# Four stacked attention layers on one core: a new order of a grouped-query layer's rounds, one moved copy in the layer behind it, and shorter moments

## The reference

```
x = L0(ctx, x)   # latent: keys and values from ctx and x, 16 heads of 32, rmsnorm, MLP
x = L1(x, ctx)   # grouped query: 32 query heads, 8 key heads of 16; layer norm behind; no MLP
x = L2(x, ctx)   # cross: layer norm, 16 heads of 32, layer norm, MLP
x = L3(ctx, x)   # latent again
# L1:
q = hidden @ Wq + bq; k = ctx @ Wk + bk; v = ctx @ Wv + bv
attn = softmax(q @ k.T / 4 + mask)
x = (attn @ v) @ Wo + bo + hidden
return (x - mean(x)) * rsqrt(var(x) + 1e-6) * gamma + beta
```

## Time and profile before

| | |
|---|---|
| median of 3 runs | 2516.99 us (2512.34 to 2518.89) |
| the profiled execution's own time | 2515.64 us |
| its span, first to last instruction | 2513.6 us |
| PE busy, share of the span | 2425.0 us, 96% |
| DVE, ACT, POOL busy | 50%, 43%, 45% |
| mean granted clock of TensorE | 0.991 |

### The profile page before, as it was taken

The page is one execution under the profiler, slowest core; times in us unless marked ns, Lnnn a source line. Parts: engine busy times, 40 slices in busy tenths (PEclk is TensorE's granted clock), DMA queues, the critical chain, the costliest instruction groups (busy, mean ns, idle before and its releaser), DMA issues.

```text
span 2513.6 us, 49031 instructions
## 1 busy us (share of the span) xinstructions
PE 2425.0 (96%) x18400; PEld 2036.1 (81%) x18400; DVE 1256.4 (50%) x3768; ACT 1087.7 (43%) x3688; POOL 1120.8 (45%) x1972
## 2 busy tenths in 40 slices
PE   7999999999999999998898999999999999999999
PEld 6888887888888878877787888888888888788887
DVE  5565655333234676676887333233565555431332
ACT  5555554111114777777887111112555555211111
POOL 3444445600053787878997720042345433740000
PEclk9999999999999999998999999999999999999999
DMA  4221212311034233222454311031121111320100
GB/s 157 69 68 60 97 39 85 97 51 51 1 107 133 75 108 115 99 104 99 172 186 136 119 70 41 11 101 64 35 81 64 52 52 52 110 96 1 51 34 17
DMA packets 107866, 198.36 MB, mean 79 GB/s; under 512 B 9392, under 2 KB 36720, under 8 KB 104688
## 3 DMA queue, kind: packets, MB, share of 16 engines
q1 hardware_dynamic: 107632, 195.22, 23.0%
HBM read 136.47 MB, written 58.72 MB: 78 GB/s over the span
## 4 chain that ended last, share of the span: by engine, by line
PE 79%; ACT 9%; DVE 7%; POOL 4%; DMA 1%; issue 1%; SPq 0%; DVEq 0%; POOLq 0%
PE banks L327 69%; PE banks L468 5%; ACT plain_high L746 5%; PE banks L498 3%; ACT plain_low L746 2%; POOL plain_high L1414 2%; DVE plain_low L1033 1%; DVE stats L1172 1%; PE banks L522 1%; DVE rounded_low L1082 1%; ACT plain_work L730 1%; POOL plain_low L1414 1%; PE banks L359 0%; DMA plain_high<-attention_w 0%; DVE plain_work L1187 0%
## 5 line engine op out<-in xcount | busy, mean ns | idle before, releaser
L327 PE MATMUL banks<-rounded_work,rounded_low 128*128 128x512 f32 (+1 forms) x2688 | 521.1, 348 | 14.5 <-DVE rounded_low L1210 9.1
L839 ACT ACTIVATE plain_work<-banks,columns 128x512 f32<-128x512 f32 x192 | 132.4, 690 | 863.6 <-PE banks L327 863.6
L327 PEld LDWEIGHTS banks<-rounded_work,rounded_low 128*128 128x128 f32 x2688 | 432.9, 192 | 79.3 <-issue 12.5
L327 PE MATMUL banks<-rounded_work,rounded_high 128*128 128x512 f32 (+1 forms) x2400 | 482.3, 355 | 1.8 <-DMA rounded_work<-ctx_split 1.3
L327 PEld LDWEIGHTS banks<-rounded_work,rounded_high 128*128 128x128 f32 x2400 | 396.1, 191 | 67.1 <-issue 5.3
L1383 DVE CAST rounded_work<-plain_work 128x512 fp32r<-128x512 f32 x192 | 106.2, 553 | 687.3 <-ACT plain_work L839 676.6
L1414 POOL TENSOR_SCALAR plain_high<-plain_high,inv_sum 128x128 f32<-128x128 f32 (+1 forms) x768 | 296.8, 409 | 301.6 <-DVE inv_sum L1055 301.3
L327 PE MATMUL banks<-rounded_low,rounded_work 128*128 128x512 f32 x1728 | 416.2, 392 | 0.0
L327 PE MATMUL banks<-rounded_high,rounded_work 128*128 128x512 f32 (+1 forms) x1728 | 391.4, 378 | 0.0
L327 PEld LDWEIGHTS banks<-rounded_low,rounded_work 128*128 128x128 f32 x1728 | 321.4, 188 | 70.7 <-issue 4.4
L327 PEld LDWEIGHTS banks<-rounded_high,rounded_work 128*128 128x128 f32 x1728 | 309.0, 188 | 62.6 <-issue 3.0
(11 more groups left out here) (110 smaller groups left out, 3313.1 us busy)
## 6 DMA issues: line engine op xcount, KB each, us to landing
plain_work<-x SPq DMA_DIRECT2D x96, 256.0 KB, 3.0
plain_work<-mlp_w SPq DMA_DIRECT2D x96, 256.0 KB, 2.7
rounded_work<-ctx_split SPq DMA_DIRECT2D x16, 1024.0 KB, 5.8
u<-plain_work SPq DMA_DIRECT2D x48, 256.0 KB, 2.3
plain_work<-u SPq DMA_DIRECT2D x12, 1024.0 KB, 7.0
x<-plain_work SPq DMA_DIRECT2D x48, 256.0 KB, 2.3
plain_work<-attention_w SPq DMA_DIRECT2D x44, 256.0 KB, 2.6
ctx_split<-rounded_work SPq DMA_DIRECT2D x8, 1024.0 KB, 5.6
```

Of the source, the lines that this page charges most:

```text
L327: mm = pe.matmul(dst, lhs(i), rhs(j), start=first and n == 0, stop=last and n == 2, skip_group_check=True)
L839: act.activation(gelu[:, j % 2, :], bank(key), ACT.Gelu_apprx_tanh, bias=col(m.y, 28 + j)).then_inc(evac_of(key), 1)
```

## The change

What it does, by engine:

- **PE**, second layer: a projection (of the third layer's values, or an output projection) is put between each `pe_scores` and the `pe_turn_probs` behind it. `pe_keys` no longer waits for the hidden rows (`pe_rows` has moved to `pe_queries`), and `pe_values` of the third layer waits for the context, since it is now its first reader.
- **ACT and DVE**, second layer: `act_late_round` and `dve_late_round` take the place of the rounds. The copies of the turned banks come behind exp 1 on ACT, and behind maximum 3 and the first inversion on DVE. Each heads' lo part (`dve_heads`) of rounds 1 and 3 goes into the middle of a later round's maxima. DVE copies both halves of the third layer's values.
- **POOL**: `pool_again` and `pool_root` move from behind round 1's norm to behind round 2's, the biases a round earlier or later.
- **SP**: the context load (`sp_c`) moves from the head of a pair to the end of the one before, behind the stores of keys and values.
- **DVE**, third layer: both copies of turned banks follow maximum 1.
- **Moments**: L1180 and L1181 go, with the wait before them; POOL reads mean and variance from `moments`, and subtracts the mean where it added its negative.

```diff
-                wait_evac(pe, ("X", y.n, p, 0))
-                wait_evac(pe, ("X", y.n, p, 1))
+                if y.kind == LATENT:
+                    pe_rows(pe, y, p)
...
+            if y.kind == GQA and i == 0:
+                pe_rows(pe, y, p)
...
+            if y.kind == CROSS and i == 0:
+                pe.wait_ge(c_loaded, 16 * (c_index(L[1], p) + 1))
...
+        def act_late_round(act, y, p, k, turned, of, between=nothing):
+            act_exp(act, y, p, k, 0)
+            act_exp(act, y, p, k, 1)
+            act_probs(act, of, *turned, 0)
+            act_probs(act, of, *turned, 2)
+            act_exp(act, y, p, k, 2)
+            between()
+            act_exp(act, y, p, k, 3)
...
-            dve.bn_aggr(moments[:, i, :], stats[:, i, :]).then_inc(aggr_done, 1)
-            dve.wait_ge(aggr_done, rt + 1)
+            dve.bn_aggr(moments[:, i, :], stats[:, i, :]).then_inc(aggr_done if y.kind == LATENT else moments_ready, 1)
             if y.kind == LATENT:
+                dve.wait_ge(aggr_done, (B if y.n else 0) + b + 1)
...
-            else:
-                dve.tensor_scalar(neg_mean[:, i:i + 1], moments[:, i, 0:1], -1.0, None, ALU.mult)
-                dve.tensor_copy(spread[:, i:i + 1], moments[:, i, 1:2]).then_inc(moments_ready, 1)
...
+        def dve_late_round(dve, y, p, k, turned, lower, beside, behind, of):
+            dve_max(dve, y, p, k, 0)
+            dve_max(dve, y, p, k, 1)
+            lower()
+            dve_max(dve, y, p, k, 2)
+            beside()
+            dve_max(dve, y, p, k, 3)
+            dve_invert(dve, y, p, k, (0,))
+            dve_probs(dve, of, *turned, 1)
+            dve_probs(dve, of, *turned, 3)
+            behind()
+            dve_invert(dve, y, p, k, (1,))
...
+                dve_late_round(dve, y, p, 1, (p, 0), last_heads, lambda: values(0) if p else None, rows, y)
...
+                dve_late_round(dve, y, p, 2, (p, 1), cross_keys, odd_out, odd_moments, y)
...
+                dve_late_round(dve, y, p, 3, (p, 2), lambda: dve_heads(dve, y, p, 1), lambda: values(1), nothing, y)
...
+                dve_late_round(dve, *((y, p + 1) if more else (L[2], 0)), 0, (p, 3), nothing,
+                               lambda: dve_add(dve, y, 2 * p), even_moments, y)
...
-                for r in range(4):
+                for r in range(2):
                     dve_max(dve, y, p + 1, 0, r)
-                    if r % 2:
-                        dve_probs(dve, y, p, 1, r)
+                dve_probs(dve, y, p, 1, 1)
+                dve_probs(dve, y, p, 1, 3)
+                for r in range(2, 4):
+                    dve_max(dve, y, p + 1, 0, r)
...
                 pool_norm(pool, y, p, 1)
                 if p:
-                    pool_again(pool, y, 2 * p - 2)
-                    pool_root(pool, y, 2 * p - 1)
-                pool_norm(pool, y, p, 2)
-                if p:
-                    pool_again(pool, y, 2 * p - 1)
-                pool_bias(pool, y, 2 * p)
+                    pool_bias(pool, y, 2 * p - 1)
...
+                pool_norm(pool, y, p, 2)
+                if p:
+                    pool_again(pool, y, 2 * p - 2)
+                    pool_root(pool, y, 2 * p - 1)
                 pool_norm(pool, y, p, 3)
-                pool_bias(pool, y, 2 * p + 1)
+                pool_bias(pool, y, 2 * p)
...
+                if p:
+                    pool_again(pool, y, 2 * p - 1)
                 pool_root(pool, y, 2 * p)
+            pool_bias(pool, y, B - 1)
...
+                if more:
+                    sp_ahead(sp, p + 1)
+                if far:
+                    wait_filled(sp, ("V", 1, p + 1, 0))
+                    sp_c(sp, y, p + 2)
```

More of the change, by code:

```diff
@@ L1280, in dve_gqa @@
             dve.wait_ge(m_stored, 64 * GROUPS)
+            for i in range(2):
+                dve_values(dve, L[2], 0, i)
             for p in range(PAIRS):
                 more = p + 1 < PAIRS
-                def inputs():
-                    for i in range(2):
-                        dve_x(dve, *((y, p + 1) if more else (L[2], 0)), i)
-                def next_inputs():
-                    if not more:
-                        for i in range(2):
-                            dve_x(dve, L[2], 1, i)
@@ new lines, in odd_out, with odd_moments, even_moments, rows @@
+                def odd_out():
+                    if p:
+                        dve_add(dve, y, 2 * p - 1)
+                def odd_moments():
+                    if p:
+                        dve_again(dve, y, 2 * p - 2)
+                        dve_added(dve, y, 2 * p - 1)
+                def even_moments():
+                    if p:
+                        dve_again(dve, y, 2 * p - 1)
+                    dve_added(dve, y, 2 * p)
+                def rows():
+                    if more:
+                        for i in range(2):
+                            dve_x(dve, y, p + 1, i)
@@ L1299, in dve_gqa @@
+                dve_late_round(dve, y, p, 1, (p, 0), last_heads, lambda: values(0) if p else None, rows, y)
                 if more:
                     dve_keys(dve, y, p + 1, 0)
-                    dve_keys(dve, L[2], p + 1, 0)
-                dve_round(dve, y, p, 2, (p, 1), nothing)
-                if p:
-                    dve_again(dve, y, 2 * p - 1)
+                else:
+                    for i in range(2):
+                        dve_x(dve, L[2], 0, i)
+                dve_heads(dve, y, p, 0)
@@ L1313, in dve_gqa @@
                 dve_heads(dve, y, p, 2)
-                dve_round(dve, *((y, p + 1) if more else (L[2], 0)), 0, (p, 3), nothing, y)
-                next_inputs()
-                dve_out(dve, y, 2 * p)
+                dve_late_round(dve, *((y, p + 1) if more else (L[2], 0)), 0, (p, 3), nothing,
+                               lambda: dve_add(dve, y, 2 * p), even_moments, y)
                 if more:
                     dve_queries(dve, y, p + 1, 1)
-                dve_heads(dve, y, p, 3)
+                else:
+                    for i in range(2):
+                        dve_x(dve, L[2], 1, i)
+            dve_heads(dve, y, PAIRS - 1, 3)
         def dve_cross(dve, y):
@@ L1441, in pool_root @@
             pool.wait_ge(u_stored[b % 2], stored_count(y.b0 + b - 2))
[L1442 removed]
+            pool.tensor_scalar(u, h, moments[:, i, 0:1], rstd[:, i:i + 1], ALU.subtract, ALU.mult).then_inc(rooted, 1)
             if y.kind == GQA:
```

122 lines of the change are left out of this document (63 added, 59 removed).

## The result

The change makes the kernel slower by 1.0%. The prediction had 2497 us, from 2486 to 2510.

What follows compares the result with a forecast made beforehand. PE's own work was taken as the floor, so only its idle time could be won. Terms -16.8 (middle), -0.3 (first), -1.5 (last), -1.5 (third layer) sum to -20.1: 2515.64 to 2495.5, plus 1.35 for the median, 2497 us, range 2486 to 2510.

Steps and rivals of the forecast that it cites:

- the third layer's term: Seven third-layer pairs: PE's wait moves to the queries and does not go; only shorter moments gain, -1.5 us (bounds 0, -8).
- In the second layer the moments lie in DVE's slack: 0: Second layer: removing the moments' instructions L1180 and L1181 neither gains nor costs time, 0 us.
- the rivals: Late copies chain up (0.17, 2510), third layer gains -8 (0.08, 2490), context load decides (0.07, 2525), order does nothing (0.06, 2515).
- Middle pairs: Second layer's six middle pairs: 44.7 us each instead of 47.50, a gain of 2.8 six times, -16.8 us.
- ring wait of 0.7 us: Middle pairs: PE waits for banks held by copies, 0.4 at hidden rows and attention, 0.1 at third-layer keys, 0.2 rounding.
- the floor: PE's own work in a middle pair, 47.50 - 3.5 = 44.0 us, unchanged by the new order.
- The excess of 3.5 us: Time PE loses per middle pair beyond undisturbed work, mainly turned banks of rounds 2 and 3 slowed to POOL's pace.
- the sign of failure: Middle pairs above 46.5 us, with PE waiting on DVE's copies or the context load, would show the forecast wrong.
- Context load: Moved to the end of the preceding pair: lands at 41.8, first reader at 45.6, spare 3.8 us, so no cost.
- the rival of the load: Load lands too late for a pair's first projection: 3.3 us wait plus 1.4 for the clock, 2525 us; chance 0.07.
- First pair: Second layer's first pair: joined wait of 4.1 +1.0, clock +0.7, rounds 2 and 3 -2.0; sum -0.3 us.
- Last pair: Second layer's last pair: 3 us shorter at full clock, half given back for the clock, -1.5 us (bounds -5, +4).

Runs made afterwards that it cites:

- run 1: The change with the negated mean and variance copy written again and POOL adding instead of subtracting: 2505.63 us, 0.9955 of the kernel before.
- run 3: The change with POOL adding the mean from `moments` where it subtracted it, in both places: 2504.06 us, 0.9952 of the kernel before.
- run 5: The change with the added negated mean restored, plus two extra POOL additions (512 and 256 columns) before each such sum: 2558.61 us, 1.0169 of the kernel before.
- run 8: The kernel before with the second layer's new order alone, old moments and old third-layer copies: 2500.39 us, ratio 0.9938.
- run 10: Second layer's order alone, variance read from `moments`, one negation kept, early copies back in two rounds each of first and last pair: 2502.64 us, 0.9945 of kernel before.
- run 11: Second layer's order alone, with early copies in the first pair and its first attention ahead of the small keys: 2499.21 us, 0.9934 of the kernel before.
- run 7: The kernel before with the third layer's moved copies of turned banks alone: 2522.76 us, ratio 1.0019.
- run 9: Second layer's order alone, with DVE still writing the negated mean, POOL adding it and reading the variance from `moments`: 2503.03 us, 0.9943 of the kernel before.

## Why the prediction was wrong

**The step that failed** is in the last sentence of the third layer's term, "In the second layer the moments lie in DVE's slack: 0", with "POOL needs 226.02 / 6 = 37.7 us a pair and in 44.5 us finds room". The shorter moments were costed for DVE, where instructions went, and not for POOL, where one changed. Each operation's 0.76 us was taken over from the row of an addition and given to the subtraction without bounds, though no row of the trace showed one in that form. What the runs showed in its place: 1.31 us on each of 48 tiles, POOL at 254.53 / 6 = 42.4 us a pair, and +35 us (runs 1 and 3 against the change; run 5 for POOL's time as the way). POOL at 79% in the earlier trace rows had 9.8 us a pair to spare; that a slower operation there could use them up stands in none of the rivals, and what happened is outside the range and outside all of them. In the third layer there was less room still, (167.32 - 146.44) / 7 = 3.0 us a pair, of which two subtractions take 2.6, and the prediction walked only DVE there.

**Middle pairs: 44.7, right.** Runs 1 and 8 measure 44.70 without the subtraction, six times. The sum was right and its parts weren't. No ring wait of 0.7 us is left and the floor isn't 44.0: PE is busy 267.77 of 268.19 us. The floor stood in the earlier trace rows as PE's busy time, 268.56 / 6 = 44.8. The excess of 3.5 us, summed from single rows, was 0.7 too large, and a ring wait of 0.7 that isn't there made up for it: that the two cancel to the tenth is luck. In the changed kernel the pairs took 47.0 on average, over the 46.5 that was named as the sign of failure, with the wait on DVE, as that part said; but it was DVE's output sum, late through POOL, and not its copies.

**Context load: right.** PE waits for it nowhere in the middle pairs, so the rival of the load falls.

**First pair: -0.3 forecast, +2.8 (run 1) and +4.0 (run 8) measured.** The late copies were walked for the middle pairs, where a projection stands between scores and turned banks. In the first pair none does. The changed kernel:

```profile
812.77 1.09 PE L362 MATMUL banks<-ident,plain_work 128*128 128x128 f32 x8 [2.88 <-ACT plain_work L738]
814.92 2.74 PE L326 MATMUL banks<-rounded_work,rounded_high 128*128 128x256 f32 x12 [1.06 <-DMA rounded_work<-ctx_split]
...
825.74 0.66 PE L475 MATMUL banks<-ident,plain_high 128*128 128x128 f32 x4 [1.17 <-DVE rounded_low L1117]
827.92 4.29 PE L326 MATMUL banks<-rounded_work,rounded_high 128*128 128x256 f32 x22 [1.52 <-ACT plain_work L738]
```

The first wait sums with the load's to 3.9, near the 4.1 forecast, but two more of 1.2 and 1.5 follow, and the clock, 0.96 before, is 0.93. The 1.5 is for a late copy of ACT, and is gone in runs 10 and 11, which copy early there. The 1.2 is for DVE's lo part of the third layer's keys (L1117), and with early copies it is 1.8, so the late copies aren't its cause. The prediction's -2.0 for rounds 2 and 3 had no such waits in it.

**Last pair: -1.5 forecast, -1.5 in run 1** (43.96 against 45.48), -0.6 in run 8. The number is luck. The prediction had the pair 3 us shorter at full clock and gave half of that back for a lower clock. In run 1 PE's idle time grew, from 45.48 - 36.29 = 9.2 to 43.96 - 33.12 = 10.8, and its busy time fell by 3.2 at a clock of 0.92 in place of 0.85. In the change +3.1, with POOL busy 46.88 of 48.56 us.

**Third layer: -1.5 forecast, +3.9 us measured by stretch** (172.21 in run 7, 172.27 in run 1, against 168.35), +5 by medians (run 7 against the kernel before, run 1 against run 8), +17.8 in the change. The forecast's whole gain was the shorter moments, and no run shows it (runs 3 and 9). That the wait moves and doesn't go was right: 1.87 us ahead of the queries, none ahead of the attention. Two sizes were missed beside the one above. First the clock: the earlier trace rows had shown 12 matmuls of 256 columns at 2.93 us behind a wait, and I charged it in the first pair and not here. At 1.3 to 2.7 us in three or four pairs it turns the term's sign. The 48 matmuls behind a wait of 1.87 us in run 1:

```profile
1248.74:1256.10 7.36, 7.36 (x49) 7.36 (x50) 6.88 (x45) 6.07 (x29) 7.04 (x19) 0.78 0.83 327
```

The Trainium skill (TensorE: Matmul & The Clock Gate, Part 1: The HAM clock gate) says that the clock falls with idleness. The trace agrees: 0.78 is the mean over these 7.4 us, and 0.50 was granted in the 4.2 us behind the wait of 3.14 shown above. It doesn't hold behind every such wait (see the end), and the prediction quoted it at the first pair only. Second, in the change, DVE's split of the hidden rows became slower. DVE, third layer of the change (busy us, mean ns):

```profile
L1146 DVE TENSOR_TENSOR rounded_work<-plain_work,rounded_work 128x512 fp32r<-128x512 f32 x12 | 13.9, 1161 | 0.4
L1144 DVE CAST rounded_work<-plain_work 128x512 fp32r<-128x512 f32 x12 | 10.2, 852 | 0.0
```

and of the kernel before:

```profile
L1129 DVE TENSOR_TENSOR rounded_work<-plain_work,rounded_work 128x512 fp32r<-128x512 f32 x12 | 9.5, 789 | 0.4
L1127 DVE CAST rounded_work<-plain_work 128x512 fp32r<-128x512 f32 x12 | 7.9, 656 | 0.0
```

The two subtractions push POOL's own split later, onto DVE's. The pair at 1299.31, DVE:

```profile
1300.78 1.49 DVE L1144 CAST rounded_work<-plain_work 128x512 fp32r<-128x512 f32 x1
1302.30 1.63 DVE L1146 TENSOR_TENSOR rounded_work<-plain_work,rounded_work 128x512 fp32r<-128x512 f32 x1
```

and POOL:

```profile
1300.39 1.59 POOL L317 TENSOR_TENSOR rounded_high<-plain_work,rounded_high 128x512 fp32r<-128x512 f32 x1
1301.94 1.44 POOL L1475 TENSOR_TENSOR plain_work<-plain_work 128x512 f32<-128x512 f32 x1
```

In run 1 the cast that starts 0.2 us into such a POOL instruction takes 1.39 us, and the next one, beside POOL's norm, 0.41. Run 5, without a subtraction, has the slow splits too (1106 and 1009 ns), so no subtraction is needed for them; that the meeting with POOL's two-input instructions slows them is read from these durations and was not tested by itself. The Trainium skill (SBUF — State Buffer, SBUF: two separate sides) says that DVE, with two SBUF inputs or in a two-port mode, and GpSimd share one port pair, which the first to start holds for its whole instruction. The trace agrees where POOL's instruction has two inputs: each of the two DVE instructions above ends 0.3 and 0.6 us behind POOL's (1301.98 and 1303.38), about its own undisturbed length of 0.4 and 0.7. Beside the short pieces of POOL's norm the trace shows no such slowing of DVE, and it doesn't show whether the cast runs in a two-port mode.

## What to carry to other kernels

An instruction whose operation changes is a new instruction, however alike its shape is: give it a row of its own or a wide bound, on the engine that runs it, before counting what its edit saves elsewhere. On GpSimd a tensor_scalar with a subtraction took 2.07 us here against 0.76 with an addition, so negate the operand on another engine and add. Here the forecast for the steady part of the loop was as good as its busy-time floor; walk the first and last iteration anew, since what covers a wait in the middle (here a projection) isn't there.

## What the runs showed that was not expected

- **Subtraction on GpSimd.** A 128x512 tensor_scalar takes 0.76 to 0.77 us with add and mult, 2.07 to 2.08 with a subtraction in either place. It isn't so for every form: POOL's TENSOR_TENSOR that subtracts a rounded tile (L317 in the change, 1.28 us undisturbed) takes as long as the one that adds a bias (L1475, 1.26). Why the one form is slow, no run shows.
- **One wait of 1.9 us costs more than 1.2 and 0.6 apart.** The matmuls behind it took 7.3 to 8.7 us in 7 of 10 pairs of runs 1 and 7 (the second to the sixth pair of the layer, waits of 1.86 to 2.17 us), and 6.0 in the other three; behind the split wait they took 6.0 in all ten such pairs of the kernel before and of run 8. What decides isn't settled: in run 1 a pair with 1.88 was undisturbed and one with 1.86 wasn't, and in run 7 one with 2.01 was undisturbed.
